# Routed expert step: the second layer of two tiles back goes ahead of the transposes of hid, and x is taken ahead of hid

## The reference

```
h   = x through cond_weights[subject] + bias            # 4096 x 512
w, sel = route(h)                                       # 4 of 16 experts, group-limited, w sums to 2.5
out = sum over e of cw[:, e] * (silu(h @ gate[e].T) * (h @ up[e].T)) @ down[e].T
shared = silu(h @ shared_gate.T) * (h @ shared_up.T) @ shared_down.T
return x + out + shared
```

## Time and profile before

| | |
|---|---|
| runs | 827.44, 834.33 and 827.2 us, median 827.44 |
| profiled execution | 826.33 us, span of its instructions 824.5 us |
| busy in the span | PE 812.5 us (99%), PEld 649.7 (79%), DVE 485.0 (59%), ACT 388.3 (47%), POOL 433.4 (53%) |
| granted TensorE clock | 0.998 in the mean |
| DMA | 220 GB/s in the mean |
| first layer, L1111 psGU | 1716 matmuls, 415.9 us |
| second layer, L1111 psY | 564 and 282 matmuls, 187.9 and 111.4 us |
| transposes of hid, L982 psH | 284, 54.0 us |

### The profile page before, as it was taken

The page is one execution under the profiler, slowest core; times in us unless marked ns, Lnnn a source line. Parts: engine busy times, 40 slices in busy tenths (PEclk is TensorE's granted clock), DMA queues, the critical chain, the costliest instruction groups (busy, mean ns, idle before and its releaser), DMA issues.

```text
span 824.5 us, 19365 instructions
## 1 busy us (share of the span) xinstructions
PE 812.5 (99%) x4133; PEld 649.7 (79%) x4134; DVE 485.0 (59%) x1017; ACT 388.3 (47%) x782; POOL 433.4 (53%) x399
## 2 busy tenths in 40 slices
PE   9999999999999999999999999999999999999996
PEld 5578778888887888888888888888888888888874
DVE  5798899627444446644457446647557466464441
ACT  4864334535334345534455445546455355453441
POOL 5403112625567555566665665655565573765543
PEclk9999999999999999999999999999999999999999
DMA  8986969899999899899997999899998998998965
GB/s 288 394 332 177 247 149 260 204 203 268 239 251 237 177 192 176 202 276 241 182 196 185 270 216 217 210 267 189 229 266 175 282 246 198 236 206 164 198 94 68
DMA packets 145305, 181.52 MB, mean 220 GB/s; under 512 B 30570, under 2 KB 103922, under 8 KB 142834
## 3 DMA queue, kind: packets, MB, share of 16 engines
q0 software_dynamic: 37776, 89.08, 52.3%
q1 hardware_dynamic: 106528, 80.45, 38.4%
q10 hardware_dynamic: 834, 10.49, 3.6%
HBM read 82.52 MB, written 67.17 MB: 182 GB/s over the span
## 4 chain that ended last, share of the span: by engine, by line
PE 93%; DVE 3%; issue 1%; DMA 1%; ACT 1%; POOLq 0%; POOL 0%; DVEq 0%; SPq 0%; ACTq 0%
PE psGU L1111 47%; PE psY L1111 23%; PE psY L1169 5%; PE psH L982 4%; PE psGU L1152 3%; PE psGU L1154 3%; PE psGU L1153 3%; PE psT L982 1%; DMA raw_w<-ffn_w 1%; PE psY L1031 1%; PE psGU L1031 1%; PE psH L1008 1%; PE psM L1139 1%; PE psM L968 0%; DVE aT_low L1703 0%
## 5 line engine op out<-in xcount | busy, mean ns | idle before, releaser
L1111 PE MATMUL psGU<-split_w,xT_pair 128*128 x1716 | 415.9, 391 | 1.0 <-issue 1.0
L1111 PEld LDWEIGHTS psGU<-split_w,xT_pair 128*128 128x128 f32 x1716 | 321.9, 188 | 71.7 <-issue 1.9
L694 POOL DMA_INDIRECT out<-y_ring,idx_all x143 | 228.8, 1600 | 203.6 <-SPq L583 184.1
L1758 DVE SCALAR_TENSOR_TENSOR aT<-aT,w_ring,psGU 128x256 f32<-128x256 f32 x143 | 68.6, 480 | 238.6 <-ACT aT L934 216.1
L689 POOL DMA_INDIRECT tok_ring<-h_rows,idx_all x143 | 150.3, 1051 | 73.3 <-issue 42.0
L1111 PE MATMUL psY<-split_w,hidT_hi 128*128 x564 | 187.9, 414 | 0.0
L934 ACT ACTIVATE aT<-psGU 128x256 f32<-128x256 f32 x143 | 55.0, 384 | 255.2 <-PE psGU L1111 255.2
L840 ACT ACTIVATE y_ring<-psY 128x512 f32<-128x512 f32 x173 | 103.6, 599 | 101.1 <-PE psY L1111 63.3
L1111 PE MATMUL psY<-split_w,hidT_lo 128*128 x282 | 111.4, 395 | 0.0
L1111 PEld LDWEIGHTS psY<-split_w,hidT_hi 128*128 128x128 f32 x564 | 95.4, 189 | 13.5 <-issue 0.2
L1743 DVE STREAM_TRANSPOSE psT<-x_ring 128x512 f32<-128x512 f32 x143 | 102.5, 717 | 0.1
(11 more groups left out here) (268 smaller groups left out, 651.4 us busy)
## 6 DMA issues: line engine op xcount, KB each, us to landing
x_ring<-tok_ring SPq DMA_DIRECT2D x284, 128.0 KB
raw_w<-ffn_w SPq DMA_DIRECT2D x17, 1536.0 KB, 10.1
out<-y_ring POOLq DMA_DIRECT2D x32, 256.0 KB, 7.5
x_ring<-x_pairs SPq DMA_DIRECT2D x12, 512.0 KB, 8.6
h_rows<-tok_ring SPq DMA_DIRECT2D x16, 256.0 KB, 9.7
h_rows<-y_ring SPq DMA_DIRECT2D x16, 256.0 KB, 10.0
tok_ring<-h_rows,idx_all POOLq DMA_INDIRECT x143, 6.5
out<-y_ring,idx_all POOLq DMA_INDIRECT x143, 6.2
```

Source lines behind the costliest of these rows:

```text
L694: pool.indirect_dma_start(out[:, :], bass.IndirectOffsetOnAxis(idx_all[:, r:r + 1], 0), y_ring[:, r % YRING, :], None, compute_op=ALU.add) ...
L1111: mm = pe.matmul(dst, a[:, slot, c], w(at + col + k * H), start=(k == 0 and a is high and at == 0), stop=(k == parts - 1 and a is low))
L1758: v.scalar_tensor_tensor(out=hid[:, half, :], in0=gate, scalar=w_ring[:, w_slot, bass.ds(expert, 1)], in1=up, op0=ALU.mult, op1=ALU.mult). ...
```

## The change

Nothing is added or removed; three orders within a routed step are altered.

- TensorE: `down(n-2)` right behind `gate_up(n)`, then `xpose_hid(n-1)`. Only in the step before the last the old order stays.
- ScalarE: `copy_xT(n+2)` ahead of `copy_hidT(n-1)`.
- VectorE: `split_x(n+2)` and `turn_x(n+3)` ahead of `split_hid(n-1)`.

```diff
@@ scalar, step @@
-                if n != NT and n != LAST:
-                    copy_hidT(t + -1, None if n is None else n - 1)
+                if n == LAST - 1:
+                    copy_hidT(t + -1, n - 1)
                 if n is None or n < LAST - 1:
                     copy_xT(t + 2, None if n is None else n + 2)
+                if n is None or NT < n < LAST - 1:
+                    copy_hidT(t + -1, None if n is None else n - 1)
@@ tensor, step @@
                 else:
-                    xpose_hid(t + -1, None if n is None else n - 1)
-                if n is None or n >= NT + 2:
-                    down(t + -2, None if n is None else n - 2,
-                         kept[-3] if j >= 2 else weights(t + -2, None if n is None else n - 2)[0])
+                    if n == LAST - 1:
+                        xpose_hid(t + -1, n - 1)
+                    if n is None or n >= NT + 2:
+                        down(t + -2, None if n is None else n - 2,
+                             kept[-3] if j >= 2 else weights(t + -2, None if n is None else n - 2)[0])
+                    if n != LAST - 1:
+                        xpose_hid(t + -1, None if n is None else n - 1)
@@ vector, step @@
-                elif n is None or n < LAST - 1:
-                    split_hid(t + -1)
                 if n is None or n < LAST - 1:
                     split_x(t + 2)
                 if n is None or n < LAST - 2:
                     turn_x(t + 3)
+                if n is None or NT < n < LAST - 1:
+                    split_hid(t + -1)
```

## The result

| | before | changed |
|---|---|---|
| median of six runs | 827.32 us (826.11 to 834.33) | 840.45 us (837.18 to 843.85) |
| ratio, 95% interval | | 1.0156 (1.0127 to 1.0184) |
| profiled execution (its span) | 826.33 us (824.5) | 837.18 us (835.4) |
| granted TensorE clock, mean | 0.998 | 0.996 |
| waits of PE between 290 and 820 us | 1.0 us in 2 | 7.2 us in 6 |

The changed kernel is slower by 13.1 us, over 1%. The forecast was 831.5 us with a range from 827 to 837. The profiled execution happens to be the shortest of the six, and is 10.9 us longer than the profiled one of before; that part can be read off.

The account below looks back on a forecast made before the run. TensorE, busy 500.00 of 500 us, was taken as the bound. Late piece steps (1.4 and 1.0), loop entry 1.2, first steps 0.3, word loads and loop ends 0.6 made 4.5 us more: 831.5 us, range 827 to 837.

Parts of the forecast that it names:

- TensorE's own period: TensorE's routed step: moving the two transposes leaves the period at 4.36 us, so this term is 0.
- Ordinary steps: Steps without weight work: hidT_lo ready at 1.35 us of the next step, 1.25 us of cover left, no cost.
- Limit 2.6: TensorE's second layer: hidT_lo is in time until 2.6 us into the next step.
- typical piece step 2.1: Steps that also split a piece of weights: hidT_lo ready at 2.1 us of the next step, inside the limit.
- B: Rival: piece steps over the limit as a class, 836 to 839 us; chance 0.14.
- Late scalings: Nine piece steps with VectorE's scaling late: eight at 0.17 us over the limit, one at 1.0; 1.4 and 1.0 us.
- Loop entry 1.2: VectorE's entry to its loop: hidT_lo comes behind the turn of x, so TensorE's matmuls are 1.2 us later.
- first two steps 0.3: First two routed steps, where VectorE also has a copy of y: 0.3 us.
- word loads and loop ends 0.6: Word loads and loop ends that meet a late step: 0.6 us.
- The last two steps keep the old order: nothing.: End of the routed steps: the last two keep the old order and so cost nothing.

Follow-up runs that it names:

- e1: Changed order on TensorE alone, ScalarE and VectorE as in the kernel before: 831.15 us, ratio 1.0055 to before.
- e3: Changed kernel, but all three engines keep the old order in the last two steps of each turn of TensorE's loop: 834.64 us, ratio 1.0081 to before.
- e4: Kernel before, but with the changed order in the last two steps of each turn of TensorE's loop: 832.60 us, ratio 1.0070 to before.
- e7: Changed kernel, but VectorE splits hid ahead of its work on x: 830.84 us, ratio 1.0058 to before.
- e9: Changed kernel with VectorE's loop eight steps earlier, each step's work unchanged: 836.28 us, ratio 1.0119 to before.
- e5: Kernel before with TensorE's two transposes in the middle of the second layer: 828.45 us, ratio 1.0026 to before.
- e8: e1 with the old place of the transposes in the last two steps of each turn of TensorE's loop: 829.66 us, ratio 1.0041 to before.
- e10: Kernel before with hid copied ahead of the silu on ScalarE and split ahead of the scaling on VectorE: 827.30 us, ratio 1.0014 to before.

## Why the prediction was wrong, by its own steps

- **TensorE's own period.** Right to 0.02 us: 4.34 instead of 4.36. And the small gain is not the change's: in the second profile of before the period is 4.34 too (timeline of PE, below), and in that of e1 it changes from 4.353 to 4.34 behind the gap of step 111, in the middle of the run.

```profile
319.53 2.90 PE L1111 MATMUL psGU<-split_w,xT_pair 128*128 x12
...
323.87 2.89 PE L1111 MATMUL psGU<-split_w,xT_pair 128*128 x12
```

- **Ordinary steps: scaling at 3.65, hidT_lo at 1.35, cover 1.25 us.** Right (3.61, 1.33, no gap).
- **Limit 2.6, typical piece step 2.1.** Right. Piece steps whose scaling is not late lie at 1.7 to 2.3 and cost next to nothing (0.1 us in one). B's mechanism, piece steps over the limit as a class, did not happen, though its time of 836 to 839 is nearer than mine.
- **Late scalings, 2.4 us for nine.** Mechanism right, list too long. The first of them is there with 1.01 us again and its hidT_lo is ready at 2.7; it costs 0.14 us. With steps 77, 97 and 113 all of them cost 1.4 us.
- **Loop entry 1.2, first two steps 0.3, word loads and loop ends 0.6.** Measured 0.5, nothing, and about 0.4 at back edges (the loop's jumps back to its start); a word load of 1.09 us at 350.0 us cost nothing.
- **"The last two steps keep the old order: nothing."** The largest failed step, 4.45 us in the profile. The last two steps do keep it, but the step ahead of the loop's exit doesn't, and there the order decides how early the sequencer gets to its branch. The 0.7 us on "issue" in the earlier trace rows was this gap; I showed the row and didn't ask what hid the rest of a silence of 4.3 us. e3 takes the long gap away, e4 brings it in.
- **The list of late steps read from one profile.** The other failed step, 5.9 us. I took the first profile of before as the full list of what can be late. A profile in which TensorE never waits can't show how much lateness its cover hides, and the delays of a transfer or a signal differ from run to run. Step 131 is bound to its place and was on time in that one profile; the second showed it 2 us late.
- **Cover measured at one place only.** I had 1.25 us of cover as ample for ordinary steps and priced the rest by exceptions. e7 shows what counted: with the scaling at the head of the chain to hidT_lo each late scaling is passed on in full; with the copy of hid at its head, 1 us of it is absorbed. The two kernels differ by 8 to 11 us while ordinary steps look the same.
- **The clock.** No term of the sum had it. Eight gaps of 2.7 to 3.8 us were followed by matmuls at the lower level; in the changed kernel's two profiles six and twelve distances of the first layer behind the exit are 0.427 instead of 0.227 us, and step 141 takes 7.6 and 8.3 us instead of 6.0. The gap of 3.29 us in e9 was not followed by it (granted clock 1.00 from 730 to 740 us).

What isn't settled: why q8's packet at TensorE's exit starts 1.9 to 2.0 us behind the branch in seven profiles (before twice, e1, e3, e5, e8, e10) and 3.1 to 3.8 in five (changed kernel twice, e4, e7, e9). It is not the order on TensorE alone, since e1 and e7 have the same one. In the five, the last packet of the other instruction queue, q14, started 0.1 to 0.5 us ahead of the branch, in the seven it came 0.2 to 0.8 us behind it; whether the one holds up the other no run tests. Also open is what makes TensorE's results reach the others 1 to 3 us late in a few steps; and the 3 to 6 us by which the changed kernel's medians lie over its profiled runs.

## What to carry to other kernels

Cover that no wait uses is not spare: before giving half of it up, look for the places where every run is late (loop exits and entries, code behind a loop, slow transfers) and ask for each engine what its queue holds at that moment. Take two or three profiles of the kernel before, since one in which the bound engine never waits hides both the size and the list of the delays. Put on the critical chain first what others wait for; putting two instructions of x, of no hurry, behind hid again on VectorE took most of this loss away (e7).

## What the runs showed of the hardware that I had not expected

- Behind the branch that leaves TensorE's loop the next load comes 4.3 to 6.2 us later, 1.3 to 1.6 us after a 16 KB instruction packet has landed (twelve profiles). 0.7 to 1.0 us of it shows where the branch passes 0.9 us into the step, 3.2 to 3.8 us where it passes at 2.1.
- VectorE's stream has a silence three steps behind its loop's exit, 2.1 to 5.4 us of lateness in eight profiles with the exit at its old place, 0.6 in that of e5, none in the first of before and in that of e10. In e9 it moves with the exit, and a q14 packet lands 1.5 to 1.7 us before its end.
- The period of the same 20 matmuls is 4.353 us in some stretches and 4.34 in others, within one run and in the same kernel; in e1 the change comes behind a gap, in e10 without one. Over some 120 steps that is 1.6 us, which may be part of the spread between runs of before.
- Gaps of 2.70 us (e8, step 131) and 2.74 us (e7, at its exit) were followed by the lower clock, one of 1.93 us in the changed kernel and one of 3.29 us in e9 were not. The length of the gap alone does not tell.
